# Reordering one core's fused attention, MLP and pixel-attention kernel: chunk 3's first layer norm behind the first half's scaled queries, and the second half's attention gelu ahead of chunk 1's fc1 gelu

## The reference

```python
# layer 0
h   = biasfree_ln(x, ln1_w)              # x / sqrt(var over channels + 1e-5) * w
x1  = gelu(depthwise3x3(h[:, :16]))      # half of the channels
x2  = gelu(conv1x1(h[:, 16:]))           # -> q, k, v, lfeat, 8 channels each
qf, kf = avg_pool_3s2p1(q), max_pool_2s2(k)
attn = softmax(einsum('bcn,bdn->bcd', qf, kf), axis=1).swapaxes(1, 2)
out = concat([x1, lfeat, attn @ v]) + x
m   = biasfree_ln(out, ln2_w)
h   = gelu(conv1x1(m, fc1))              # 32 -> 128 channels
h   = h + gelu(depthwise3x3(h, pos))
X   = out + conv1x1(h, fc2)              # 128 -> 32
# layer 1, attention over the 256 pixels
q, k, v = Wq X, Wk X, Wv X
y   = X + softmax(q k^T, axis=1) @ v
```

## Time and profile before

| what | value |
|---|---|
| time, median of 3 runs | 112.94 us (112.91 to 114.23) |
| profiled execution | 113.05 us |
| its span, first to last instruction | 111.3 us |
| PE busy | 95.7 us (86%) |
| DVE busy | 76.3 us (69%) |
| ACT busy | 86.2 us (77%) |
| POOL busy | 11.7 us (11%) |

### The profile page before, as it was taken

The page is one execution under the profiler, slowest core; times in us unless marked ns, Lnnn a source line. Parts: engine busy times, 40 slices in busy tenths (PEclk is TensorE's granted clock), DMA queues, the critical chain, the costliest instruction groups (busy, mean ns, idle before and its releaser), DMA issues.

```text
span 111.3 us, 5328 instructions
## 1 busy us (share of the span) xinstructions
PE 95.7 (86%) x2424; PEld 53.9 (48%) x2424; DVE 76.3 (69%) x155; ACT 86.2 (77%) x203; POOL 11.7 (11%) x25
## 2 busy tenths in 40 slices
PE   0097699999969999989987999999999999997660
PEld 0023286865425567324443653576624665585320
DVE  0002997554749897999879889567471789889751
ACT  4048897797989639896569899869999868979950
POOL 7010000000000000000000003692000030004200
PEclk9999999999999999999999999999999999999998
DMA  2991053200000000000000000000000200020022
GB/s 53 229 377 52 0 219 112 119 0 6 6 0 9 0 9 6 0 6 6 0 6 0 6 6 0 0 6 6 6 0 6 94 0 6 0 93 4 0 95 99
DMA packets 2070, 4.56 MB, mean 41 GB/s; under 512 B 384, under 2 KB 640, under 8 KB 2048
## 3 DMA queue, kind: packets, MB, share of 16 engines
q1 hardware_dynamic: 1904, 4.20, 10.6%
q10 hardware_dynamic: 144, 0.03, 0.2%
HBM read 1.96 MB, written 1.05 MB: 27 GB/s over the span
## 4 chain that ended last, share of the span: by engine, by line
PE 62%; ACT 22%; DVE 6%; DMA 4%; issue 3%; ACTq 0%; DVEq 0%
PE ps L398 19%; ACT prob L787 5%; PE ps L488 5%; ACT hpad L738 5%; PE ps L446 4%; DMA first<-first_in 4%; PE ps L498 4%; PE ps L518 4%; PE ps L481 3%; ACT prob L774 3%; PE ps L415 3%; PE ps L286 3%; PE ps L382 3%; PE ps L423 2%; ACT swapped L733 2%
## 5 line engine op out<-in xcount | busy, mean ns | idle before, releaser
L398 PE MATMUL ps<-hpad,third 32*32 32x450 f32 (+2 forms) x864 | 38.9, 563 | 0.1
L787 ACT ACTIVATE prob<-ps,smax 128x256 f32<-128x256 f32 x56 | 25.7, 477 | 3.8 <-DVE smax L999 3.7
L952 DVE SCALAR_TENSOR_TENSOR unit<-hpad,third,unit 128x544 f32<-128x544 f32 x32 | 23.5, 789 | 0.0
L999 DVE TENSOR_REDUCE smax<-ps 128x2 f32<-128x512 f32 x26 | 16.6, 685 | 4.7 <-PE ps L498 2.9
L398 PEld LDWEIGHTS ps<-hpad,third 32*32 32x32 f32 x864 | 15.1, 103 | 8.7 <-issue 4.5
L263 POOL TENSOR_TENSOR v_tok<-v_tok,row_inv 128x256 f32<-128x256 f32 x7 | 4.7, 677 | 87.8 <-DVE row_inv L1009 87.8
L787 ACT ACTIVATION_READ_ACCUMULATOR prob<-ps,smax 128x1 f32 x56 | 11.7, 209 | 0.0
L738 ACT ACTIVATE hpad<-ps,third 128x1024 f32<-128x1024 f32 x8 | 8.7, 1116 | 2.9 <-PE ps L382 2.4
L879 DVE SCALAR_TENSOR_TENSOR npad<-x,first,rstd 128x256 f32<-128x256 f32 x8 | 3.5, 480 | 10.3 <-ACT rstd L716 10.3
L518 PE MATMUL ps<-prob,v_tok 128*32 128x256 f32 x128 | 8.2, 383 | 2.3 <-ACT prob L774 1.1
L707 ACT ACTIVATE swapped<-ps 128x512 f32<-128x512 f32 x8 | 4.5, 593 | 7.2 <-PE ps L286 7.2
(11 more groups left out here) (87 smaller groups left out, 145.1 us busy)
## 6 DMA issues: line engine op xcount, KB each, us to landing
prob<-npad SPq DMA_DIRECT2D x4, 297.5 KB, 2.5
x<-x_in SPq DMA_DIRECT2D x4, 256.0 KB, 5.6
y<-m SPq DMA_DIRECT2D x3, 256.0 KB, 2.5
third<-third_in SPq DMA_DIRECT2D x1, 456.5 KB, 6.8
second<-second_in SPq DMA_DIRECT2D x1, 401.5 KB, 5.8
y<-m SPq DMA_DIRECT2D x2, 128.0 KB, 2.0
first<-first_in ACTq DMA_DIRECT2D x1, 33.0 KB, 4.9
```

The costliest lines, as they stand in the source:

```text
L398: last = pe.matmul(inside(pixels(ps[quadrant(rotated(r, g)), banks[g], :]), tap), c3("taps")[quadrant(r), tap * C:(tap + 1) * C], inside(p ...
L787: last = act.activation(prob[:, G * (slot_turn(s) % PROBS) + g, jt * NPIX:(jt + 1) * NPIX], ps[:, banks[q], jt * NPIX:(jt + 1) * NPIX], AC ...
L952: dve.scalar_tensor_tensor(out=sums, in0=source, scalar=weight, in1=sums, op0=ALU.mult, op1=ALU.add).then_inc(unit_step, 1)
L999: dve.tensor_reduce(smax[:, s, 2 * q:2 * q + 2], ps[:, banks[q], :].rearrange("p (j i) -> p j i", j=2), AX_X, ALU.max, negate=True).then_i ...
```

## The change

On ScalarE `inverse_root(0, 3)` (Ln and Exp of chunk 3) stands after `scale_queries(0)` in place of ahead of the first half's `qk_act`, and `attn_act(2)`, `attn_act(3)` stand ahead of `hidden(1, ...)`. On VectorE chunk 3's `normalise_input` and `split_parities` stand after the first half's `softmax_in`, and `conv_steps` are cut at other places. On TensorE the single taps of half 0 are issued in parts by slots, `channel_scores(0)` writes banks 4 and 5 and stands ahead of all pairs, all pairs of half 1 stand ahead of chunk 1's fc1, which is done by whole matmuls, and mix, centring, variance and the taps of chunk 1 are in another order. The activations and table loads stay the same in number. Chunk 1's fc1 is 4 matmuls in place of 16 (8 and 32 instructions).

```diff
-            def attn_singles(H, lo, hi, banks):
+            def attn_singles(H, lo, hi, banks, slots=range(G)):
...
-                    for t in range(G):
+                    for t in slots:
@@ TensorE, first half
             centre(0, 3, HIGH)
+            pe.wait_ge(second_loaded, 16)
+            pe.wait_ge(normed[0], 2)
+            attn_singles(0, 0, 2, LOW, (0, 1))
             variance(0, 2, HIGH)
             variance(0, 3, HIGH)
-            pe.wait_ge(second_loaded, 16)
-            pe.wait_ge(normed[0], 4)
-            attn_singles(0, 0, 1, LOW)
+            attn_singles(0, 2, 3, LOW, (0, 1))
             pe.wait_ge(log_ready[0], 3)
             qk(0, 4)
             qk(1, 4)
-            attn_singles(0, 1, 3, LOW)
+            pe.wait_ge(normed[0], 4)
+            attn_singles(0, 0, 2, LOW, (2, 3))
             pool_queries(0, 5)
-            attn_pairs(0, 0, 1, LOW)
+            attn_singles(0, 2, 3, LOW, (2, 3))
+            pe.wait_ge(kf_zeroed, 1)
+            channel_scores(0, (4, 5))
+            attn_pairs(0, 0, 3, LOW)
             pe.wait_ge(log_ready[0], 4)
-            pe.wait_ge(kf_zeroed, 1)
-            channel_scores(0, (5, 6))
-            attn_pairs(0, 1, 3, LOW)
             qk(2, 7)
             qk(3, 7)
             mix(0, LOW)
@@ TensorE, second half and chunk 1
             fc1_all(0, LOW)
-            attn_pairs(1, 0, 1, HIGH)
+            attn_pairs(1, 0, 3, HIGH)
             pe.wait_ge(normed[1], 2)
             pe.wait_ge(hid_gelu, 1)
-            fc1_by_tiles(1, 0, 0)
-            fc1_by_tiles(1, 1, 1)
-            attn_pairs(1, 1, 2, HIGH, (2, 3))
+            fc1(1, 0, 0)
+            fc1(1, 1, 1)
             pe.wait_ge(hid_gelu, 2)
-            fc1_by_tiles(1, 2, 2)
-            fc1_by_tiles(1, 3, 3)
-            attn_pairs(1, 1, 2, HIGH, (0, 1))
-            attn_pairs(1, 2, 3, HIGH)
+            fc1(1, 2, 2)
+            fc1(1, 3, 3)
+            pe.wait_ge(attn_gelu, 4)
+            mix(1, HIGH)
 
             pe.wait_ge(hid_gelu, 3)
             conv_taps(1, 0, 1, LOW, (0, 1))
+            pe.wait_ge(res1_ready, 3)
+            centre(1, 2, HIGH)
             pe.wait_ge(hid_gelu, 4)
             conv_taps(1, 0, 1, LOW, (2, 3))
-            pe.wait_ge(attn_gelu, 4)
-            mix(1, HIGH)
-            conv_taps(1, 1, 3, LOW)
-            pe.wait_ge(res1_ready, 3)
-            centre(1, 2, HIGH)
             pe.wait_ge(res1_ready, 4)
             centre(1, 3, HIGH)
-            conv_taps(1, 3, 4, LOW)
+            conv_taps(1, 1, 2, LOW)
             variance(1, 2, HIGH)
             variance(1, 3, HIGH)
-            conv_taps(1, 4, 7, LOW)
+            conv_taps(1, 2, 5, LOW)
             pe.wait_ge(log_ready[1], 4)
             pe.wait_ge(normed[1], 3)
             for g in range(G):
                 fc1(2, g, HIGH[g])
-            conv_taps(1, 7, 9, LOW)
+            conv_taps(1, 5, 9, LOW)
@@ ScalarE
             inverse_root(0, 2, HIGH)
-            inverse_root(0, 3, HIGH)
             act.preload_act_table_set(gelu_tables)
             qk_act(0, 4)
             act.preload_act_table_set(exp_tables)
             scale_queries(0, 5)
+            inverse_root(0, 3, HIGH)
             channel_exp(0)
...
             hidden(0, 2, (2, 3))
+            attn_act(2, HIGH)
+            attn_act(3, HIGH)
             hidden(1, 0, (0, 1))
             hidden(1, 2, (2, 3))
-            attn_act(2, HIGH)
-            attn_act(3, HIGH)
@@ VectorE
-            for k in range(CHUNKS):
+            for k in range(CHUNKS - 1):
                 dve.wait_ge(x_loaded[k], 16)
                 normalise_input(k)
...
             pool_keys(0)
-            softmax_in(0, (5, 6))
+            softmax_in(0, (4, 5))
+            dve.wait_ge(x_loaded[3], 16)
+            normalise_input(3)
+            split_parities(3)
             dve.wait_ge(blocks_zeroed, 1)
             dve.wait_ge(mix_preset, 1)
             softmax_out(0)
...
-            conv_steps(0, 8)
+            conv_steps(0, 5)
             residual(2, HIGH)
             residual(3, HIGH)
-            conv_steps(8, 13)
+            conv_steps(5, 11)
             normalise(2)
-            conv_steps(13, 14)
+            conv_steps(11, 13)
             normalise(3)
-            conv_steps(14, 25)
+            conv_steps(13, 25)
```

## The result

The changed kernel is faster, by less than was forecast. From 20 executions of each the ratio of after to before is 0.994, 95% interval 0.9915 to 0.9965, which is 0.4 to 1.0 us; the medians are 112.56 (after) and 113.56 us (before). The ratios leave out executions more than 1.5% above the same kernel's fastest, and with them all above 120 us: over all sets these were 24 of 168 with the old order of place A (before, place B only, before with early matmuls) and none of 110 with the new one. The change lies within 2%, as forecast, and within the range, but the forecast was 0.94 us off a base of 112.94, which is a ratio of 0.9917, at the very edge of the interval; its middle is 0.68 us. A second measurement of the changed kernel, with another set of executions, gave 0.9957 (0.9919 to 0.9996), or 0.5 us.

What follows compares the result with a forecast made beforehand. Neither TensorE's convolution taps (19% of the chain) nor ScalarE's evictions bound it alone; they hand work to each other. 113.05 - 0.35 - 0.6 = 112.1, with the median 0.1 below the profiled execution, 112.0 us; range 111.0 to 113.1.

Steps and rivals of the forecast that it cites:

- place A: 12 to 25 us: chunk 3's Ln/Exp moved behind the scaled queries gains 0.35 us, bounds 0 and 0.75.
- place B: 30 to 50 us: reordered gelus, pairs and taps; squares 3.0 us earlier, gain 0.6 us.
- One cost I had put at nothing: 32 new tap instructions of slots 0 and 1 ahead of the variances: cost nothing, at most 0.7 us.
- Rival (a): Taps cost 31 to 35 ns; only the first place's gain or part of the second's survives: 112.6; chance 0.21, shared.
- keep its distances: Behind chunk 3's first fc1, forecast at 48.8 instead of 49.74: what follows keeps its distances.
- Rival (b): More gain: place A keeps 0.75 us and taps go at 25 ns: 111.0 us or less; chance 0.12.
- Rival (c): Slower: TensorE's clock falls in place B, low level held from 34 to 38.7: 113.7 us; chance 0.07.
- The two more changes between tiled and whole matmuls: Around chunk 1's fc1: 1.0 us on the path by the draining rule, none in the hole before the mix.

Runs made afterwards that it cites:

- place B only: Only the edits of place B, with place A as before, against the kernel before: ratio 0.9969.
- before with early matmuls: Kernel before plus eight 128x128 float32 matmuls on zeroed data while TensorE waits for the first input: ratios 0.997 and, repeated, 0.9957 to the kernel before.
- place A again: Second run of only the edits of place A, the rest as before, against the kernel before: ratio 0.9973.
- tiled fc1: Changed kernel with chunk 1's fc1 in 32 tiled matmul instructions, behind all the pairs: ratio 0.9901 to the kernel before.
- tap in the hole: Changed kernel with one tap of chunk 2 moved into TensorE's idle time ahead of chunk 3's first fc1: ratio 0.9999 to the kernel before.
- early matmuls: Eight 128x128 matmuls on zeroed data while TensorE waits for the first input; in the changed kernel ratios 0.9885 and, repeated, 0.9958 to the kernel before.
- variances first: Changed kernel with the single taps of slots 0 and 1 behind chunk 2's and chunk 3's variances: ratio 1.0007 to the kernel before.
- place A only: First run of only the edits of place A, the rest as before, against the kernel before: ratio 0.9946; its trace had gelu 0 at 26.29.
- before, again: Kernel before, unedited, traced a second time and timed against itself: ratio 0.9999.

## Why the forecast was too large: the price of TensorE's stretch ahead of chunk 2's fc1

**Place A, forecast 0.35: held on average, with some luck.** Gelu 0 is at 25.26, 25.52 and 25.65 with the old order (before twice, place B only), and at 24.99, 25.03, 25.06, 25.14 and 25.36 with the new (changed twice, place A again, tiled fc1, tap in the hole): means 25.48 and 25.12, so 0.36. Left aside are early matmuls, the late clock (26.29) and variances first, which is an order of its own. The chain went as drawn: first gelu of queries/keys 0.9 earlier (forecast 1.0), small exp 0.9 (1.0), attention gelu 0.9 (1.0), second gelu 0.27 to 0.54 (0.35), the rest returned at VectorE's split and softmax_out. Luck is in the number: the forecast started from the quickest of the old traces, and against that one (25.26) the new order gains 0.14 on average. One cost I had put at nothing: Ln of chunk 2 is 0.23 later by the early taps at the high level. With TensorE at the low level it is 1.5 later than in before, but only 0.5 of that is time in which the variances had not begun (1.16 less 0.63), which is within the bound that I gave (0.7).

**Place B, forecast 0.6: the step that failed.** The prediction priced the stretch from the first of the three taps ahead of chunk 2's fc1 to that fc1 at 2.85 + 0.45 = 3.3 us, as 96 instructions at 29.5 ns each and the gap behind the last tap. The 29.5 ns are those of one uninterrupted row of 92, and the four instructions ahead of it, which run among the variances, were priced like the rest. The trace of before itself has them, just ahead of the row at 41.86 in the earlier trace rows:

```profile
41.45 0.71 PE L398 MATMUL ps<-hpad,third 32*32 32x480 f32 x4
41.63 0.42 PE L297 MATMUL ps<-swapped,first 32*32 32x256 f32 x8
```

From 41.45 to fc1 at 45.03 it is 3.58 us, not 3.3. In the eight traces with the new place B it was 3.47 to 3.87, 3.66 in both of the changed kernel. The stretch began 7.98 to 8.49 us after gelu 0 where 8.1 was forecast, 8.39 in the changed kernel's first trace, so some is lost before it too, where taps, centring and variances are mixed. Behind fc1 nothing varies: conv gelu follows it by 5.26 to 5.28 us in all eight (forecast 5.4). Over the six without early matmuls (changed twice, place B only, variances first, tap in the hole, tiled fc1) the means add up: 8.20 + 3.59 + 5.27 = 17.06 against the forecast's 8.1 + 3.3 + 5.4 = 16.8.

The same row of taps ahead of fc1, TensorE, in the changed kernel's second trace, then place B only:

```profile
39.03 3.47 PE L398 MATMUL ps<-hpad,third 32*32 32x480 f32 x92
42.43 1.14 PE L376 MATMUL ps<-m,third 32*128 32x512 f32 x8
```

```profile
39.31 3.19 PE L398 MATMUL ps<-hpad,third 32*32 32x480 f32 x92
42.43 1.14 PE L376 MATMUL ps<-m,third 32*128 32x512 f32 x8
```

By the prediction's own formula these are (3.47 - 0.56)/91 = 32.0 and 28.9 ns. The matmuls themselves are as long in both, as the profile models them (561 ns on average). What differs is how they start: in bunches, mostly under 20 ns apart, with pauses of 0.12 to 0.20 us between the bunches, nine such pauses in the first row and seven in the second.

Gelu 0 to conv gelu is 17.32, 17.05, 16.77, 17.05, 16.87 and 17.32 in the six, and 16.74 and 17.63 with early matmuls. With the old order it was 17.36 to 17.38 in all six. So place B is worth 0.31 on average, and from 0.6 to a loss of 0.25 in one execution. The forecast's 0.6 is its upper end, reached twice (place B only and the changed kernel's first trace with early matmuls), and there by errors that cancel: the stretch took 3.53 and 3.49 and not 3.3, and what stands before and behind it 0.1 less each.

**Why the new order varies and the old one never did stays open.** Up to the squares both are alike: each time ScalarE's and VectorE's results set TensorE going again, and the squares come 6.60 or 6.61 us after gelu 0 in six of the eight traces of the new place B. The scatter arises behind them, up to fc1. The old order has the same work there and its fc1 came 14.05 to 14.07 after gelu 0 in all six traces. It isn't that slack swallowed the pauses: there too ScalarE waited for that fc1, and from its gelus went on to the convolution gelu at 48.33 without idle time. In before:

```profile
46.23 2.12 ACT L738 ACTIVATE hpad<-ps,third 128x1024 f32<-128x1024 f32 x2 [0.50 <-PE ps L376]
```

No pause of the new kind was seen there at all. What did change is who is waited for last: ScalarE's gelus before, the taps now (1.95 idle before L745). Rival (a), "taps cost 31 to 35 ns, so TensorE's stream returns the rest", had this right in place and size. From the first to the last of the 96 instructions the new traces have 31.4 to 35.5 ns each, the old one 32.7. The small groups that it blamed are part of it, the uninterrupted row the other.

**The tail.** The prediction let everything behind conv gelu "keep its distances". It did: from there to the end it is 62.88 to 63.32 us in thirteen of the fourteen traces, of either order. The fourteenth is the second trace of before, with 63.76 by the standstill shown above.

**Together** the traces give 0.36 + 0.31 = 0.67 us at the end of place B, and the timing 0.68 (0.4 to 1.0) and 0.5 (0.05 to 0.9). Forecast was 0.95. The split between the places rests on the traces; the ratios of the kernels with one place only (0.9946 and 0.9973, 0.9969) are too wide to give it. Rival (b), more gain at 25 ns, never occurred. Rival (c), a fall of the clock in place B, did not occur in any trace of the changed order. The two more changes between tiled and whole matmuls cost nothing, as forecast: the squares are earlier with them than without (6.60 against 6.86); the 0.49 from last tap to fc1 stood again (39.03 + 3.47 - 0.56 = 41.94 to 42.43).

## What to carry to other kernels

Price a stretch of matmuls from its first start to the next step's, as the trace has it (3.58 us here), and not by the rate of its cleanest row (3.3). Take that price from several executions, since the engine that a reorder leaves on the path brings its own scatter. Before crediting a milestone to an edit, subtract when the first input landed: here 0.6 of 0.92 us. An idle stretch ahead of a matmul group isn't room for more work if the next step waits for the group's end: one tap moved there cost 0.4 us. And work moved ahead of a dependent step "into idle time" is free only at the speed at which that engine runs there.

## What the runs showed of the hardware that I had not expected

**When the clock rises is chance.** Of matmuls with 256 columns the last one slower than 550 ns started at 8.3 us (place B only), 8.7, 9.3, 9.3, 9.7, 9.8, 9.9, 10.0, 10.6 and as late as 13.8 us (place A only), in kernels whose TensorE program up to there was the same or nearly so; soon after they took 370 to 400. Eight early 128x128 matmuls between 1.3 and 5.0 us brought it to the first centring in three executions of four, and to the second group of centring in the fourth. In the profile's granted clock the stretch before the rise reads 1.00 all the same; only the durations show it. The Trainium skill, TensorE: Matmul & The Clock Gate, Part 1, calls the number of slow matmuls at the start run-variable; the traces agree.

**A fall with TensorE busy.** In the second trace of before with early matmuls the granted clock fell to half at 13 us and stayed there to 37. The windows of that execution (PE busy, PEld, DVE, ACT, POOL, then the granted clock) and of the first trace of before:

```profile
13.00:37.00 24.00, 23.80 (x480) 17.25 (x454) 10.61 (x36) 13.36 (x21) 0.00 (x0) 0.50 0.14 53
```

```profile
13.00:37.00 24.00, 22.34 (x685) 13.87 (x688) 16.75 (x47) 21.23 (x30) 0.00 (x0) 1.00 0.14 55
```

480 matmul instructions were issued where 685 were, at 1.2 GHz in place of 2.4, and the span is 119.3 us. TensorE was busy for 23.80 of the 24 us, so the low level held without its being idle; before the fall it did centring, variances and the first taps, with a pause of 1.92 us ahead of the variances at 11.2. Other traces have such a pause of 1.45 (before), 1.61 (before, again), 1.70 (variances first) and 1.78 us (place B only) and no fall. Why it fell in this execution and not in the others stays open.

**Standstills of TensorE** for which the profile names only "issue", of 0.20 to 0.59 us, stand in six of the fourteen traces, one in each, at different places of executions that otherwise agree to 0.01 us. No run tested where they come from.
